# Mixture-of-experts layer: first expert tile before the last shared tiles, shared sums written from another queue, table order rotated, gathers without a bounds check

## What is computed

```
x = x + layernorm(attention(layernorm(x)))
xt = layernorm(x)                                 # 2048 tokens x 512
probs = softmax(xt @ router_w.T); top 8, weights normalised to sum 1
routed = sum over e of weight_e * ((silu(xt @ Wg_e.T) * (xt @ Wu_e.T)) @ Wd_e.T)
shared = sigmoid(xt @ Wse.T) * ((silu(xt @ Wsg.T) * (xt @ Wsu.T)) @ Wsd.T)
x = x + layernorm(routed + shared)
```

## Time and profile before

| | |
|---|---|
| median of three runs | 1158.32 us (1157.26 to 1160.17) |
| the profiled execution | 1158.39 us, of which the span from first to last instruction is 1156.6 us |
| PE busy | 1067.8 us, 92% |
| POOL busy | 609.7 us, 53% |
| DVE busy | 671.0 us, 58% |
| ACT busy | 503.8 us, 44% |
| gathers L472 | 7 by `token_i`, 152 by `idx`, 1045 ns each on average |
| scatters L478 | 157, 1592 ns each on average |

### The profile page before, as it was taken

One profiled execution on the slowest core, in us unless ns is written; L12 is line 12 of the kernel. 1 busy time (PEld: TensorE's weight loads), 2 busy tenths in 40 slices (PEclk: granted clock), 3 DMA queues, 4 the chain that ended last, 5 costly groups with the idle time before them and its releaser, 6 DMA issues.

```text
span 1156.6 us, 24273 instructions
## 1 busy us (share of the span) xinstructions
PE 1067.8 (92%) x6269; PEld 721.7 (62%) x6270; DVE 671.0 (58%) x2307; ACT 503.8 (44%) x1418; POOL 609.7 (53%) x632
## 2 busy tenths in 40 slices
PE   6999899989999989989899999999999999999954
PEld 3555566555566645556677776776777777767721
DVE  5666566556666668869734444444545454445538
ACT  2666567656666654446532222222222222222214
POOL 3433334333433313311338888787878887888710
PEclk9999999999999999999899999999999999999978
DMA  9700000000000033110458999999999999998788
GB/s 320 292 2 1 3 1 1 1 3 1 1 1 1 2 115 159 55 37 1 150 168 193 221 227 238 236 238 241 253 224 256 237 233 277 267 222 169 117 279 319
DMA packets 66295, 166.73 MB, mean 144 GB/s; under 512 B 15394, under 2 KB 17186, under 8 KB 66096
## 3 DMA queue, kind: packets, MB, share of 16 engines
q0 software_dynamic: 38512, 83.95, 32.7%
q1 hardware_dynamic: 27712, 81.88, 20.2%
HBM read 119.85 MB, written 62.65 MB: 158 GB/s over the span
## 4 chain that ended last, share of the span: by engine, by line
PE 56%; DMA 23%; DVE 10%; issue 6%; POOL 3%; ACT 1%; DVEq 1%; POOLq 0%; SPq 0%
PE ps L756 15%; DMA sum_rows<-x_t,idx 14%; PE ps L1025 8%; DMA x_t<-x_rows,idx 7%; PE ps L815 7%; PE ps L873 4%; PE ps L785 4%; PE ps L1036 4%; PE ps L835 4%; PE ps L1009 2%; PE ps L770 2%; POOL x_t L472 2%; DVE low L1314 2%; DVE qkv_all L1318 1%; POOL sum_rows L478 1%
## 5 line engine op out<-in xcount | busy, mean ns | idle before, releaser
L1025 PE MATMUL ps<-big,work 128*128 x1264 | 299.0, 379 | 0.0
L478 POOL DMA_INDIRECT sum_rows<-x_t,idx x157 | 249.9, 1592 | 58.7 <-issue 36.0
L1025 PEld LDWEIGHTS ps<-big,work 128*128 128x128 f32 x1264 | 227.9, 190 | 25.2 <-issue 0.8
L472 POOL DMA_INDIRECT x_t<-x_rows,idx x152 | 158.9, 1045 | 46.3 <-issue 28.3
L756 PE MATMUL ps<-big 128*128 128x384 f32 x512 | 181.3, 498 | 2.1 <-ACT big L544 1.7
L397 POOL TENSOR_TENSOR work<-qkv_all,rope_sb 128x256 f32<-128x256 f32 x64 | 46.6, 729 | 244.7 <-ACT qkv_all L549 244.7
L697 ACT ACTIVATE work<-ps 128x512 f32<-128x512 f32 x159 | 95.0, 597 | 180.9 <-PE ps L1009 180.9
L1036 PE MATMUL ps<-big,work 128*128 x314 | 160.5, 593 | 0.0
L1009 PEld LDWEIGHTS ps<-ident_sb,x_t 128*128 128x128 f32 x636 | 77.1, 141 | 105.4 <-issue 64.6
L1145 DVE CUSTOM_DVE_ANT_0 ps<-ps,mask_sb 128x128 f32<-128x128 f32 (+3 forms) x256 | 120.7, 513 | 23.7 <-PE ps L785 23.0
L568 ACT ACTIVATE work<-ps,neg_max 128x128 f32<-128x128 f32 (+3 forms) x256 | 132.5, 528 | 3.3 <-DVE neg_max L1145 2.2
(11 more groups left out here) (186 smaller groups left out, 1454.6 us busy)
## 6 DMA issues: line engine op xcount, KB each, us to landing
big<-experts SPq DMA_DIRECT2D x65, 768.0 KB, 7.2
sum_rows<-x_t POOLq DMA_DIRECT2D x4, 2048.0 KB, 15.7
big<-sum_rows SPq DMA_DIRECT2D x8, 768.0 KB, 9.9
x_rows<-work SPq DMA_DIRECT2D x16, 256.0 KB, 2.0
out<-x_sb SPq DMA_DIRECT2D x16, 256.0 KB, 5.5
x_sb<-x SPq DMA_DIRECT2D x3, 1024.0 KB, 9.7
x_t<-sum_rows SPq DMA_DIRECT2D x4, 768.0 KB, 13.4
attn_t<-sum_rows SPq DMA_DIRECT2D x4, 768.0 KB, 13.6
```

What stands on the lines that cost most here:

```text
L472: pool.indirect_dma_start(rows[q], None, x2_rows, bass.IndirectOffsetOnAxis(ap=at, axis=0), bounds_check=last_row, oob_is_err=False).then_ ...
L478: pool.indirect_dma_start(all_sums, bass.IndirectOffsetOnAxis(ap=idx[:, q, 1:2], axis=0), y_sb[q], None, bounds_check=last_sum, oob_is_err ...
L1025: mm = pe.matmul(ps[:, 2 + p, 0:GATEUP], rows_t[:, p, c, :], w_ring[:, slot, c * GATEUP:(c + 1) * GATEUP], start=(c == 0), stop=(c == DC - 1))
```

## The change

Line numbers of the changed kernel differ by up to ten from those of the kernel before.

**POOL and SP.** `keep_shared` moves from POOL's program into SP's. It writes tiles 0 to 5, then 6 to 12, then, behind the load of the eighth expert's weights, 13 to 15, all counted on `s_ysh`. POOL now zeroes all three tables. Scatter c goes to table (c + 1) % 3, so table 0 is first used by the third scatter, before which DVE waits for `s_ysh`.

**Gathers.** The gathers have no bounds check. DVE clamps their indices to 2047 with a `min`: for the first eight tiles in one added instruction (`first_i`), later inside the instruction that copied the index anyway. Slots without a token, which were skipped, now fetch row 2047; their results are still dropped by the scatter, whose index is not clamped.

**PE, ACT and DVE.** The late shared tiles have buffers of their own. The order of the late tiles and the first expert tiles is written anew, up to `down(0)` ahead of the last shared tile. The loop body is the same cycle, begun one step later. PE's register loads move into the early tiles (i == 9). Tile 15's gate and up results and its down result use PSUM bank 7, which holds the table until DVE has read it.

```diff
@@ sync
+            def keep_shared(lo, hi):
+                sp.wait_ge(s_sy, hi)
+                sp.dma_start(sums_v[0][:, lo:hi, :], y_shared[:, lo:hi, :]).then_inc(s_ysh, 16)
+            sp.wait_ge(s_scatter[0], 32)
+            keep_shared(0, 6)
+            keep_shared(6, EARLY)
             sp.wait_ge(s_sdn, TILES)
             sp.dma_start(w_ring[:, NW - 1, :], experts[NW - 1]).then_inc(s_wl[NW - 1], 16)
+            keep_shared(EARLY, TILES)
...
@@ gpsimd
-            for p in range(1, TABLES):
+            for p in range(TABLES):
                 for half in range(2):
                     pool.dma_start(sums_v[p][:, 8 * half:8 * half + 8, :],
...
             def gather(q, at):
                 pool.indirect_dma_start(rows[q], None, x2_rows,
-                                        bass.IndirectOffsetOnAxis(ap=at, axis=0), bounds_check=last_row,
-                                        oob_is_err=False).then_inc(s_gather[q], 16)
+                                        bass.IndirectOffsetOnAxis(ap=at, axis=0)).then_inc(s_gather[q], 16)
...
-            keep_shared(11, TILES, s_scatter[0])
-            pool.wait_ge(s_ysh, 16)
...
-                pool.wait_ge(s_scatter[c % TABLES], (j * 2 + (c // TABLES + 2)) * 16)
+                pool.wait_ge(s_scatter[table_of(c)], (j * 2 + (c // TABLES + 2)) * 16)
...
@@ tensor
+                if i == 9:
+                    pe.wait_ge(s_tables, 4)
+                    quads = pe.value_load(pairs_i[0:1, 1:2], min_val=(B * S * K // P + DEEP - 2) // DEEP,
+                                          max_val=(HIGH + DEEP - 2) // DEEP)
+                    load_slots(0)
...
             shared_down(12)
+            turn_rows(0, 0, 16)
+            shared_up(15)
+            pe.wait_ge(s_late, 2)
+            up(0, 0, slot_of(0))
             shared_turn(13)
-            shared_up(15)
-            turn_rows(0, 0, 16)
+            turn_rows(1, 1, 16)
             shared_down(13)
             shared_turn(14)
-            turn_rows(1, 1, 16)
+            pe.wait_ge(s_shte, TILES - 1)
+            turn_hidden(0, 0)
+            up(1, 1, slot_of(1))
             shared_down(14)
-            pe.wait_ge(s_late, LATE - 1)
-            up(0, 0, slot_of(0))
+            pe.wait_ge(s_sy, TILES - 1)
+            down(0, 0, slot_of(0))
             shared_turn(15)
             turn_rows(2, 2, 16)
+            pe.wait_ge(s_late, LATE)
             shared_down(15)
...
@@ vector
-            tokens(0, HEAD).then_inc(s_head, 1)
+            step(tokens(0, HEAD))
+            dve.tensor_scalar(first_i[:, :], token_i[:, 0:HEAD], B * S - 1, None, ALU.min).then_inc(s_head, 1)
...
-                dve.tensor_scalar(idx[:, q, 0:1], token_i[:, bass.ts(t, 1)], 0, None, ALU.add).then_inc(s_idx, 1)
+                dve.tensor_scalar(idx[:, q, 0:1], token_i[:, bass.ts(t, 1)], B * S - 1, None, ALU.min).then_inc(s_idx, 1)
...
-                dve.wait_ge(s_scatter[q % TABLES], r)
-                dve.tensor_scalar(idx[:, q, 1:2], token_i[:, bass.ts(t, 1)], (q % TABLES) * B * S, None, ALU.add)
+                dve.wait_ge(s_scatter[table_of(q)], r)
+                if q == 2:
+                    dve.wait_ge(s_ysh, 48)
+                dve.tensor_scalar(idx[:, q, 1:2], token_i[:, bass.ts(t, 1)], table_of(q) * B * S, None, ALU.add)
```

More of the change, by code:

```diff
@@ L447, in _ @@
                                        op=ALU.add).then_inc(s_prefix, 1)
-            def keep_shared(lo, hi, done):
-                pool.wait_ge(s_sy, hi)
-                pool.dma_start(sums_v[0][:, lo:hi, :], y_shared[:, lo:hi, :]).then_inc(done, 16)
             for i in range(EARLY):
@@ L480, in scatter @@
                                         compute_op=ALU.add).then_inc(s_scatter[p], 16)
-            last_row = pool.to_reg(B * S - 1)
             last_sum = pool.to_reg(TABLES * B * S - 1)
@@ L489, in _ @@
                                    max_val=(HIGH + DEEP - 2) // DEEP - 1)
-            keep_shared(6, 11, s_ysh)
             pool.wait_ge(s_sgu, EARLY)
@@ L518, in _ @@
             pool.wait_ge(s_y, full * DEEP + (DEEP + 1))
-            pool.wait_ge(s_scatter[0], (full * 2 + 4) * 16)
+            pool.wait_ge(s_scatter[table_of(0)], (full * 2 + 4) * 16)
             pool.sem_inc(s_issue, 1)
@@ L529, in _ @@
             for p in range(TABLES):
-                pool.wait_ge(s_scatter[p], (full * 2 + (5 if p == 0 else 4)) * 16)
+                pool.wait_ge(s_scatter[p], (full * 2 + (5 if p == table_of(0) else 4)) * 16)
                 pool.sem_inc(s_issue, 1)
@@ L707, in _ @@
             shared_y(12)
+            turned(0, 0)
+            shared_gate(15)
+            silu(0, 0)
             shared_hidden(13)
-            shared_gate(15)
-            turned(0, 0)
+            turned(1, 1)
             shared_y(13)
             shared_hidden(14)
-            turned(1, 1)
+            silu(1, 1)
             shared_y(14)
-            act.wait_ge(s_late, LATE - 1)
-            silu(0, 0)
             shared_hidden(15)
@@ L916, in shared_turn @@
                     pe.wait_ge(s_log, TILES)
[L917 removed]
+                h = hidden[:, i % 2, :] if i < EARLY else late_hidden[:, i - EARLY, :]
+                pe.transpose(ps[:, 4, 0:P], h, ident_sb[:, :]).then_inc(s_sht, 1)
             def shared_down(i):
                 pe.wait_ge(s_shte, i + 1)
[L921 removed]
+                if 1 <= i < TILES - 1:
                     pe.wait_ge(s_sy, i)
[L923 removed]
+                h = hidden_t[:, i % 2, :] if i < EARLY else late_turned[:, i - EARLY, :]
+                pe.matmul(ps[:, 7 if i == TILES - 1 else 5, :], h, w_ring[:, NW - 1, DC * GATEUP:WCOLS],
                           start=True, stop=True).then_inc(s_sdn, 1)
@@ L988, in _, with load_slots, slot_of @@
             place_rows()
+            slots_at = [pe.alloc_register(f"weights_slot{k}") for k in range(DEEP + 2)]
+            def load_slots(j):
+                pe.load(slots_at, ring_i[0:1, bass.ts(j, 1), :].rearrange("o j k -> o (j k)"))
+            def slot_of(k):
+                return pe.snap(slots_at[k], min_val=0, max_val=NW - 1)
             for i in range(1, EARLY):
@@ L1010, in turn_rows @@
                 mm.then_inc(s_xg_ps, 1)
-            slots_at = [pe.alloc_register(f"weights_slot{k}") for k in range(DEEP + 2)]
-            def load_slots(j):
-                pe.load(slots_at, ring_i[0:1, bass.ts(j, 1), :].rearrange("o j k -> o (j k)"))
-            def slot_of(k):
-                return pe.snap(slots_at[k], min_val=0, max_val=NW - 1)
             def up(t, p, slot):
@@ L1066, in _ @@
                     t = j * DEEP + (c + 1)
-                    down(t - 1, c % 2, slot_of(c))
                     turn_rows(t + 2, (c + 3) % DEEP, (j + (1 + (c + 3) // DEEP)) * 16)
@@ L1070, in _ @@
                     up(t + 1, c % 2, slot_of(c + 2))
+                    down(t, (c + 1) % 2, slot_of(c + 1))
                 load_slots(j + 1)
-            down(quads * DEEP, 0, slot_of(0))
             for n, i in enumerate(SUM_ON_PE):
@@ L1415, in _ @@
             stage_gather(DEEP + 1, 1)
-            for p in range(1, TABLES):
+            for p in range(TABLES):
                 dve.wait_ge(s_scatter[p], 32)
-            dve.wait_ge(s_scatter[0], 16)
-            dve.wait_ge(s_sht, TILES)
-            dve.wait_ge(s_sdn, TILES)
             with dve.Fori(0, quads) as j:
```

63 lines of the change are left out of this document (27 added, 36 removed).

## The result

The changed kernel takes 1146.21 us (median of five runs, 1143.27 to 1150.07), the kernel before 1157.26 beside it: a ratio of **0.9907** (95% interval 0.989 to 0.9925), 11 us faster. Run again later with six runs, it gave 1148.21 and 0.9928 (0.9911 to 0.9946). The likeliest time, 1139, was missed by 7 us. The time lies in the range, in the case "gather hardly faster, 1142 to 1149". But that case took the start as forecast and the gather as nearly unchanged; here the start fell short and the gather gained more. That the two errors sum to a time inside the case is luck.

What follows compares the result with a forecast made beforehand. POOL was taken to pace the routed loop at 3.24 us a tile. Profiled 1158.4, less 22 down to the floor set by PE, plus 2 for late gathers, gives 1138.4, say 1139 us; range 1134 to 1152.

Steps and rivals of the forecast that it cites:

- gather hardly faster, 1142 to 1149: Rival: the unchecked gather saves little or nothing, POOL stays the bound and only the start moves; chance 0.33.
- PE's pace: Likeliest case: the routed loop runs at PE's 3.14 us a tile instead of POOL's 3.24, 1135 to 1142; chance 0.45.
- The walk through the hand-over: PE's new order with loop durations, from the table's end: first result 586.2, loop entered at 587.6 instead of 590.99.
- 569.5, that end I keep: Start of the hand-over walk: the table's end stays at 569.5, up to 0.4 earlier or 1.6 later.
- ACT must copy y 13 and hidden 14 ... about 1.0.: Hand-over walk: ACT's copies before hidden 0 may be turned, about 1.0 us; up 1 and down 14 then end at 584.6.
- ACT's copy of y 14, 0.7.: Hand-over walk: this copy, 0.7, and down 0, 0.86, give the first expert's result at 586.2.
- POOL's chain begins 10.5 us earlier: Hand-over: first scatter at 588.0 instead of 598.49, called sure to within 2 us.
- 0 to 1.9; I take 1.0: Third scatter, first on table 0: DVE's wait for SP's last shared sums costs PE this many us.
- A saving of s a gather: Unchecked gathers shorten POOL's chain by 151 x s; bounds 0 and 0.16 us, PE's pace reached at s = 0.08.
- More rows: Empty slots now fetch 3968 rows, 9.1 MB, 25 us of all DMA engines' time; loop share 1.02, just fits.
- the full DMA engines: Rival: DMA engines, full at a share of 1.06, bound the loop at 3.24 to 3.3 us a tile; 1149 to 1157, chance 0.12.
- the repeated row: Rival: reads of one row, up to 128 times in a gather, queue behind each other; 1162 and up, chance 0.07.

Runs made afterwards that it cites:

- e5: Changed kernel without the table rotation (scatter c to table c % 3, so DVE waits for the shared sums before the first result): 1154.67 us.
- e11: Changed kernel with PE's register reads put back ahead of the late tiles: 1149.06 us, ratio 0.9903 to 0.9954.
- e7: Changed kernel with another hand-over order: ACT's register reads in the early tiles, PE's order closed up, shared down 14 in bank 6: 1145.83 us.
- e9: Changed kernel with SyncE sending the shared sums of tiles 13 to 15 ahead of the eighth expert's weights: 1146.18 us.
- e1: Changed kernel with the bounds check back on every gather, indices still clamped so all rows are moved: 1151.97 us.
- e2: Changed kernel with the old gathers (checked, indices not clamped, empty slots skipped), leaving the hand-over and tables: 1154.90 us.
- e3: Changed kernel with each empty slot reading a row of its own partition instead of row 2047, same bytes: 1147.65 us.
- e6: e3 with no bounds check on the scatters either; empty slots are added into extra rows that nothing reads: 1149.68 us.
- e8: e7 with e6's edit, the other hand-over and unchecked scatters together: 1151.32 us.
- e4: Kernel before with only its gathers changed (no check, indices clamped), old hand-over and tables: 1150.85 us.

## Why the prediction was right and wrong

**Direction and range: right.** POOL paces the loop, the change touches both its step and its start, and no other engine took over. The likeliest case, PE's pace, did not come.

**The walk through the hand-over: the step that failed.** It gave the loop's entry as 587.6; it was 590.57. By its own points:
- *The table's end, "569.5, that end I keep".* The first late tile started at 570.40, and the first gather at 572.72 instead of 571.6: PE turned its rows 1.0 late. Over the fourteen profiles that gather starts anywhere from 570.3 to 573.8. e5, which changes nothing ahead of it, has 570.33, and e11, with the register reads back in their old place, 572.59. So this 1.0 can't be put down to the change, and no walk from one profile is good to 1 us.
- *"ACT must copy y 13 and hidden 14 ... about 1.0."* ACT's own register read in `turned(1)` was left out: 1.1 us more. The word that PE reads was costed, ACT's three were not.
- *"ACT's copy of y 14, 0.7."* The copy took its 0.7, but it began only at 587.02, when down 14's last instruction had ended (1.02 us for the 0.86 counted), and PE came on 0.2 after it. With small steps D0 lost another 0.5.
- The rest is small steps. e7 takes most of these waits out, and D0 ends at 583.9: the walk's 586.2 was possible, only not in this order.

**"POOL's chain begins 10.5 us earlier": right in kind, wrong in what it counts.** The first scatter came at 591.03 and, in the second profile, 593.82, for a forecast of 588.0 called sure to within 2 us. That is 7.5 us earlier in the first, but a scatter needs a result. Before, POOL's first scatter was 6.3 us behind the first result (592.2), so it had a backlog and its chain ran at once. An earlier start can only use up that backlog. After it POOL runs at PE's heels until the fourth scatter, and that one came 5.6 us earlier, not 9.8 (588.0 + 3 x 3.14 + 1.0 = 598.4 was forecast). Here lie 4.2 of the 7.6 us by which the last scatter is later than forecast (in the second profile 6.9 of 8.4).

**The third scatter, "0 to 1.9; I take 1.0".** The prediction's own rows give 0 to 1.4 for PE (597.3 less 593.9 less the 2 us of slack), and 0.8 to 3.4 for VectorE's wait. VectorE waited 0.84 and 0.89 us in the changed kernel's two profiles, and PE, whose cost this was to be, lost nothing; it was POOL's chain that lost 0.7, which the walk had not seen. In seven variants with the same wait VectorE stood for 1.4 to 5.3 us, in three of them more than 3.4. The Trainium skill ("DMA: Bandwidth & Descriptors", anatomy of one DMA) has a sum that makes 3.8 us of such a write, as the prediction said; it is fitted to DMAs that GpSimd issues, and these are SyncE's. These runs show 6 to 11 behind a weight load. For the transfers sent ahead of it in e9 the page's sum gives an estimate of 3.2 and 2.6 us, and they took 2.8 and 2.2. So it holds about for a write with nothing ahead of it in its queue; behind another the measurement decides.

**"A saving of s a gather": the weakest step, as it said.** s is 0.058 by the gather's own duration and 0.048 by the loop, not 0.08. PE's pace, 3.13, was not reached; POOL stays at 3.19. That is the other 3.4 us. By the sign that the prediction had given for it (below 0.96 us PE's pace, 1.04 us 1148) 0.987 lies between its cases. But by the prediction's own formula 10.5 + 151 x 0.058 is 19.3 us, which is 1139 again: knowing s would not have mended the forecast. Against the 12.4 measured, 4.9 of the difference is the start's 10.5, and 2.0 is that the loop gave 6.8 for 151 x 0.058 = 8.8.

**More rows, the full DMA engines, the repeated row: right as far as the runs tell.** 9.1 MB were added, the share was 0.97 (1.02 forecast, at a faster pace), e1 against e2 shows no price, and e3 shows that a row fetched again and again costs nothing measurable. That 1.02 fits is not settled by e6 and e8, and 1.06 is not "what full looks like": two stretches of 5 us in the changed kernel's profiles read 1.09 and 1.08. By the Trainium skill ("SBUF — State Buffer", bandwidth pools), the estimate was 6.3 us hidden by the lead of six tiles; no run here could show such a delay, and none contradicts it.

**The zeroing of the third table and PE's register loads: nothing against it.** Neither shows ahead of the first gather: it starts at 572.21 in e4, which zeroes two tables and keeps the old reads, inside the spread of the others.

## What to carry to other kernels

Where one engine issues a chain at its own pace, look for the first link that it does not wait for: an earlier start moves the end only by the backlog that it had there. Walk a new order through every engine with its scalar and register reads, not only its tile work. And a wait that looks short in one profile, behind a DMA queued after a large one, can be several times as long in the next variant: put the small transfer first.

## What the runs showed of the hardware

- The bounds check of an indirect DMA costs POOL 0.058 us in a gather of 128 rows (1.045 against 0.987), and nothing in an accumulating scatter (1.594 both ways). Whether a gather's rows are really skipped does not change it (1.044 both ways).
- The same 768 KB write by one queue, behind a weight load of 768 KB and beside gathers, was waited for 6 to 11 us after its issue, in ten profiles of nine kernels; twice in the same kernel, it was 6.4 and 6.3.
- A register read from SBUF by ACT took 0.33 us in the median and 1.26 at worst (159 of them).
